# One-head attention of layer 1: batch 0 started inside the last dense steps of layer 0, batches 1 to 3 prepared between its steps

## The reference, cut to what matters

```python
# layer 0, dense part: 8 experts of hidden size 512, top 2 by router, all computed for all tokens
h = gelu(einsum('td,edh->eth', xf, W1) + b1[:, None, :], approximate=False)
expert_out = einsum('eth,ehd->etd', h, W2) + b2[:, None, :]
x = x + einsum('etd,te->td', expert_out, weights)
# layer 1, attention with one head of 128
n = _layernorm(x)
Q = n @ W_q + b_q; K = ctx @ W_k + b_k; V = ctx @ W_v + b_v
x = x + softmax(Q @ K.T * 128 ** -0.5) @ V
# layer 1, dense part: 9 experts of hidden size 256, begins with another _layernorm(x)
```

## Time and profile before

| | before |
|---|---|
| median of 3 runs | 1169.02 us |
| the profiled execution: its own time | 1170.76 us |
| the profiled execution: its span | 1169.0 us |
| mean granted clock of TensorE | 0.908 |
| busy share of the span: TensorE, VectorE, ScalarE, GpSimd | 82%, 53%, 48%, 34% |
| from the first product with keys to the first hidden product of L1f | 350.67 to 380.71 us |

### The profile page before, as it was taken

One profiled execution on the slowest core, in us unless ns is written; L12 is line 12 of the kernel. 1 busy time (PEld: TensorE's weight loads), 2 busy tenths in 40 slices (PEclk: granted clock), 3 DMA queues, 4 the chain that ended last, 5 costly groups with the idle time before them and its releaser, 6 DMA issues. The chain is left out here.

```text
span 1169.0 us, 20619 instructions
## 1 busy us (share of the span) xinstructions
PE 960.7 (82%) x7766; PEld 808.3 (69%) x7766; DVE 621.5 (53%) x1703; ACT 556.4 (48%) x1069; POOL 393.3 (34%) x386
## 2 busy tenths in 40 slices
PE   4888899999997999978898874889377876299992
PEld 3666789999976899955665654889245554288882
DVE  7885421111145443377878765345398775444443
ACT  2665444444435434445666550665345543155552
POOL 4443200100013101410101345356465557545552
PEclk9999899999997999998989895899779986599997
DMA  9999900000000000000000001766200001445543
GB/s 349 189 189 188 205 1 1 2 1 1 1 1 1 1 1 1 1 1 1 2 2 2 19 20 50 229 189 206 81 1 2 1 1 41 146 145 168 172 151 108
DMA packets 70577, 83.83 MB, mean 72 GB/s; under 512 B 5297, under 2 KB 57528, under 8 KB 70352
## 3 DMA queue, kind: packets, MB, share of 16 engines
q1 hardware_dynamic: 64336, 71.98, 25.5%
q0 software_dynamic: 4992, 8.45, 2.1%
q10 hardware_dynamic: 1152, 2.10, 0.5%
HBM read 52.15 MB, written 32.18 MB: 72 GB/s over the span
## 5 line engine op out<-in xcount | busy, mean ns | idle before, releaser
L2283 ACT ACTIVATE hT<-PS,par 128x512 f32<-128x512 f32 x200 | 136.7, 688 | 179.2 <-PE PS L2231 177.6
L2323 DVE SCALAR_TENSOR_TENSOR X<-PS,wts,X 128x128 f32<-128x128 f32 x272 | 76.6, 344 | 226.4 <-PE PS L2243 226.3
L1092 ACT ACTIVATE hT<-PS 116x512 f32<-116x512 f32 (+1 forms) x192 | 102.0, 561 | 103.7 <-PE PS L865 102.4
L865 PE MATMUL PS<-par,score 128*116 128x128 f32 x704 | 109.7, 293 | 24.7 <-DVE oc L996 12.9
L2243 PEld LDWEIGHTS PS<-regA,hT 128*128 128x128 f32 x1024 | 119.2, 192 | 2.8
L2243 PE MATMUL PS<-regA,hT 128*128 128x128 f32 x1024 | 119.4, 275 | 0.0
L865 PEld LDWEIGHTS PS<-par,score 128*116 128x116 f32 x704 | 81.0, 143 | 42.2 <-issue 31.7
L1162 POOL TENSOR_TENSOR score<-score,mx 128x1232 f32<-128x1232 f32 x32 | 72.0, 2251 | 91.1 <-DVE mx L976 91.1
L1997 PE MATMUL PS<-q_up,halves 128*112 128x256 f32 (+1 forms) x276 | 85.6, 310 | 8.8 <-DVE hT L2106 8.8
L2229 PE MATMUL PS<-x_up,w_halves 128*128 128x512 f32 x200 | 86.4, 432 | 0.0
L1069 ACT ACTIVATE score<-score 128x1232 f32<-128x1232 f32 x64 | 78.3, 1223 | 11.8 <-POOL score L1162 9.5
(11 more groups left out here) (313 smaller groups left out, 2021.3 us busy)
## 6 DMA issues: line engine op xcount, KB each, us to landing
regA<-L3f_w SPq DMA_DIRECT2D x23, 704.0 KB, 4.1
regB<-L2f_w SPq DMA_DIRECT2D x23, 578.0 KB, 4.1
L2f_sorted_x<-empty_row SPq DMA_DIRECT2D x8, 1161.0 KB, 20.0
L3f_sorted_x<-empty_row SPq DMA_DIRECT2D x8, 1161.0 KB, 19.5
regA<-L0f_w SPq DMA_DIRECT2D x4, 768.0 KB, 16.9
regA<-L2f_sorted_x SPq DMA_DIRECT2D x23, 129.0 KB, 3.7
regB<-L3f_sorted_x SPq DMA_DIRECT2D x23, 129.0 KB, 4.0
par<-params SPq DMA_DIRECT2D x1, 2450.0 KB, 13.9
```

What stands on the lines that cost most here:

```text
L865: last = nc.tensor.transpose(PS[0:BW, bank_of(("exps", 3 * u + i)), (j % 4) * P:(j % 4) * P + P], exps_of(u)[:, first:first + BW], ident)
L1092: nc.scalar.activation(hT[0:BW, u % 2, i, 0:width], PS[0:BW, bank, 0:width], ACT.Copy).then_inc(pT_ready.sem, 1)
L2283: nc.scalar.activation(hT[:, n % 2, k, :], PS[:, i % 4, :], c["act"], bias=pc(f"{tag}_b1")[:, col:col + 1]).then_inc(h_ready.sem, 1)
```

## The change

Batch 0 is turned ahead of `output(30)` and projected after it. Batch 1 is turned and projected behind the first product with keys, batch 2 in two parts inside the step of batch 0, batch 3 in the step of batch 1. The wait for all four projections is gone, and the projections get four banks (2, 3, 6, 7) instead of two in turn. Of the norm, VectorE still applies groups 0 and 1, now ahead of the statistics in `vector_staggered`; groups 2 and 3 are applied on GpSimd, each behind its reciprocal root. `projections_vector` is no longer called for layer 1. On ScalarE the copies and the projections' evictions of groups 2 and 3 move in between the steps of the attention. Layers 2 and 3 keep their order.

```diff
             def vector_staggered(v, st, g):
                 statistics, apply = vector_functions(v, st)
+                if on_pool and 0 < g < 3:
+                    apply(g - 1)
                 if g < NG:
                     statistics(g)
-                if g:
+                if g and not on_pool:
                     apply(g - 1)
             def pool(p, st):
                 for g in range(taken if before == "attention" else 0, NG):
                     pool_group(p, g)
+                    if on_pool and g >= 2:
+                        p.wait_ge(rstd_ready.sem, rstd_ready.at(g + 1))
+                        for t in range(TG * g, TG * g + TG):
+                            nc.gpsimd.tensor_scalar(xn[:, t, :], X[:, t, :], mv[:, t, 0:1], rstd[:, 0, t:t + 1],
+                                                    ALU.subtract, ALU.mult).then_inc(xn_late.sem, 1)
             def transpose_group(pe, g, at=None):
-                pe.wait_ge(xn_ready.sem, xn_ready.at(TG * (g + 1)))
+                if on_pool and g >= 2:
+                    pe.wait_ge(xn_late.sem, xn_late.at(TG * (g - 1)))
+                else:
+                    pe.wait_ge(xn_ready.sem, xn_ready.at(TG * (g + 1)))
...
             def bank(i):
-                return {"L1x": 2 + i % 2, "L2x": (0 if i < 4 else 4) + i % 2, "L3x": 4 + i % 2}[tag]
+                return {"L1x": (2, 3, 6, 7)[i % 4], "L2x": (0 if i < 4 else 4) + i % 2, "L3x": 4 + i % 2}[tag]
...
-                    elif i >= 2:
+                    elif i >= 2 and tag != "L1x":
                         pe.wait_ge(q_used.sem, q_used.at(i - 1))
...
# single_stage, TensorE
                 scores(0)
+                nm["transpose_group"](pe, 1)
+                pj["tensor_group"](pe, 1)
                 for b in range(B):
+                    if b == 0:
+                        nm["transpose_group"](pe, 2)
                     if b + 1 < B:
                         scores(b + 1)
-                    if b == 0:
-                        pe.wait_ge(q_ready.sem, q_ready.at(B))
                     pe.wait_ge(exp_ready.sem, exp_ready.at(b + 1))
                     for j in range(TG):
                         last = nc.tensor.transpose(PS[0:K, 2 + b % 2, j * P:j * P + P], score[:, b % 2, j, :], ident)
                     last.then_inc(pT_psum.sem, 1)
+                    if b == 0:
+                        pj["tensor_group"](pe, 2)
+                    if b == 1:
+                        nm["transpose_group"](pe, 3)
+                        pj["tensor_group"](pe, 3)
...
# single_stage, ScalarE
                 exps(0)
+                nm["scalar_group"](a, 2)
                 for b in range(B):
                     a.wait_ge(pT_psum.sem, pT_psum.at(b + 1))
                     nc.scalar.activation(hT[0:K, b % 2, 0, :], PS[0:K, 2 + b % 2, :], ACT.Copy).then_inc(pT_ready.sem, 1)
+                    if b == 0:
+                        pj["scalar_group"](a, 2)
+                    if b == 1:
+                        nm["scalar_group"](a, 3)
+                        pj["scalar_group"](a, 3)
...
# ffn_stage, TensorE
                     if n + 1 < steps:
                         hidden(n + 1)
+                    woven = tag == "L0f"
+                    if woven and n == steps - 2:
+                        after_nm["transpose_group"](pe, 0)
                     output(n)
...
-                    if after_nm and n - (steps - NG) >= 2:
+                    if woven and n == steps - 2:
+                        after_nm["project_group"](pe, 0)
+                    if not woven and n - (steps - NG) >= 2:
                         after_nm["transpose_group"](pe, n - (steps - NG) - 2)
-                if after_nm:
+                if not woven:
                     after_nm["tensor_end"](pe)
...
# the list of stages, layer 1
+                        def scalar_head(a, st, nm=nm, pj=pj):
+                            nm["scalar_group"](a, 0)
+                            pj["scalar_group"](a, 0)
+                            nm["scalar_group"](a, 1)
+                            pj["scalar_group"](a, 1)
+
+                        add(dict(scalar=scalar_head, pool=nm["pool"]))
```

More of the change, by code:

```diff
@@ L505, in norm_stage @@
             rstd_ready = sem("rstd", NG)
-            xn_ready = sem("xn", NT)
+            xn_ready = sem("xn", NT - 2 * TG if tag == "L1x" else NT)
             xT_psum = sem("xT_psum", NG)
@@ L513, in norm_stage @@
             shift_ready = sem("minus_mean_by_rstd", NG if on_scalar else 0)
+            on_pool = tag == "L1x"
+            xn_late = sem("xn_late", 2 * TG if on_pool else 0)
             minus_mean, shift = scales[:, 0, :], scales[:, 1, :]
@@ L1191, in attention_stage, with single_stage @@
             return dict(tensor=tensor, vector=vector, scalar=scalar, pool=pool, pool_keys=pool_keys, pool_key_halves=pool_key_halves, pool_spread=pool_spread, x_done=x_done)
-        def single_stage(tag, q_ready, kv, after_nm):
+        def single_stage(tag, q_ready, kv, after_nm, nm, pj):
             scores_ready = sem("scores", B)
@@ L2528, in build @@
                     norm_after_ffn["tensor_end"] = lambda pe, nm=nm, pj=pj: projections_tensor(pe, nm, pj)
-                    add(dict(scalar=lambda a, st, nm=nm, pj=pj: projections_scalar(a, nm, pj),
-                             vector=lambda v, st, nm=nm, pj=pj: projections_vector(v, st, nm, pj), pool=nm["pool"]))
+                    norm_after_ffn["project_group"] = pj["tensor_group"]
+                    if layer == 1:
+                        def scalar_head(a, st, nm=nm, pj=pj):
[4 more added lines that the diff above has]
+                        add(dict(scalar=scalar_head, pool=nm["pool"]))
+                    else:
+                        add(dict(scalar=lambda a, st, nm=nm, pj=pj: projections_scalar(a, nm, pj),
+                                 vector=lambda v, st, nm=nm, pj=pj: projections_vector(v, st, nm, pj), pool=nm["pool"]))
                 if layer >= 2:
@@ L2537, in build @@
                 else:
-                    at = add(single_stage(tag, pj["ready"], kv, next_norm))
+                    at = add(single_stage(tag, pj["ready"], kv, next_norm, nm, pj))
             x_dones.append(at["x_done"])
```

## The result

The changed kernel takes 1162.21 us, the median of seven runs (1159.82 to 1165.25), against 1167.74 for seven runs of the kernel before (1166.87 to 1169.91): a ratio of 0.9946 with an interval of 0.9932 to 0.9960. It is 5.5 us faster. The profiled execution took 1160.29 us, its span is 1158.5.

What follows compares the result with a forecast made beforehand. The prediction saw the chain of norm and projections between dense layer and attention, with no engine full, as what could be saved. Terms +0.9, −5.9, +0.4 and +0.4 made −4.2, from 1169.02 to 1164.8 us; range 1162.4 to 1167.9.

Steps and rivals of the forecast that it cites:

- projection 0 ahead of the last dense addition: Before `output(31)`: projection 0's two matmuls delay the last dense addition by 0.9 us, between 0.4 and 1.0.
- the rest of the way to batch 0: From last dense addition to batch 0's addition to X: the new order saves 5.9 us.
- turning and projection 3 in batch 1: In batch 1's attention step: turning 3 and projection 3 give back 0.4 us of the gain.
- batches 2 and 3, L1f's norm: Behind batch 1: batch steps stay at 4.36 us, and L1f follows in chain from batch 3; no change.
- the clock's return in L1f: At L1f's first hidden products: arriving earlier, TensorE's clock may return late, losing 0 to 2.3 us; 0.4 taken.
- A premise: From attention to L1f: all of L1f follows in chain from batch 3, so time saved there is saved at the end.
- The clock falling for one stretch at the seam: Between dense layer and attention: half clock costs 1.9 us, leaving gain 2.3, 1166.7 us; chance 0.25.
- GpSimd was not late: Rival for GpSimd's groups at the seam: a 1.4 us hold less 0.4 cover, gain 3.2, 1165.8 us; chance 0.06.
- The third rival: Batch 3's transposes and products escape half clock, and 0.4 is not lost later: gain 5.5, 1163.5 us; chance 0.11.
- The fourth rival: Clock falls at the seam until L1f, exposing 8 us of TensorE work: 3.8 slower, 1172.8 us; chance 0.06.

Runs made afterwards that it cites:

- b4: Kernel before with only the four projection banks and the dropped waits, no order changed; ratio 0.9985 to the kernel before.
- a4: Changed kernel with turning 0 and projection 0 issued behind the last dense output; median 1168.41 us, ratio 0.9999 to the kernel before.
- a3: Changed kernel with groups 2 and 3 applied on VectorE, none on GpSimd; median 1167.80 us, ratio 0.9985 to the kernel before.
- b3: Changed kernel with unread spare products on TensorE, seven in L1f's norm and three in the attention; ratio 0.9934 to the kernel before.
- b2: Changed kernel with two extra row sums on VectorE ahead of the additions of batch 3; ratio 0.9935 to the kernel before.
- a2: Changed kernel with the exp table loaded earlier, behind the eviction of projection 0; 1165.27 us, ratio 0.9974 to the kernel before.
- b1: Kernel before, nothing edited, run for a second trace; ratio 1.0003 to the kernel before.
- d1: Changed kernel with ScalarE applying group 3 of L1f's norm ahead of the copies of group 2; median 1177.17 us, ratio 0.9912 to the kernel before.
- c3: Kernel before, nothing edited, run for a third trace; a single execution of 1166.16 us.

## Why the prediction was right or wrong

**The mechanism was right.** The order at the seam is what gained: the projections behind one another were the cost, the waits and banks were not (b4). With the early start undone batch 3 came 2.05 later (a4), with GpSimd's applies undone 3.05 later (a3). The two were undone one at a time, and what they gain may overlap. The weaving of batches 1 to 3 was never undone alone, so its share is not shown.

**The failed step is the sum, with terms mis-sized on one side.** By the distances from step 28:

| term | predicted | measured |
|---|---|---|
| projection 0 ahead of the last dense addition | +0.9 | +0.87 (16.75 to 17.62) |
| the rest of the way to batch 0 | −5.9 | −6.21 (14.43 to 8.22) |
| turning and projection 3 in batch 1 | +0.4 | +0.27 (4.36 to 4.63) |
| batches 2 and 3, L1f's norm | 0 | 0 |
| the clock's return in L1f | +0.4 | +0.12 (130.79 to 130.91) |
| sum | −4.2 | −4.95 |

Each is off by 0.03 to 0.31, and all to the same side. The two largest are the way to batch 0 and the clock's return.

On the way to batch 0 the chain is the one that was foretold, and every leg is a little shorter. Counted from the last dense addition, the eviction of batch 1 ends at 3.79 (foretold 3.9), exp 0 at 5.56 (5.7), the copy of the transposes begins at 6.31 (6.5), and X is reached at 8.22 (8.5).

The term for the clock's return had a wrong price, and this is the step whose reason failed and not only its size. It charged half of the time by which the clock would come back late. The first 6.29 us of L1f, before and changed:

```profile
380.71:387.00 6.29, 5.98 (x26) 4.75 (x27) 5.21 (x17) 4.02 (x6) 2.42 (x3) 0.75 0.01 1
374.86:381.15 6.29, 6.29 (x25) 5.24 (x26) 5.21 (x17) 4.10 (x6) 2.41 (x3) 0.63 0.00 0
```

That is 3.15 and 4.65 us at half clock: the clock did come back 1.5 us later against L1f, for which the prediction's rule charges 0.75, and the layer took only 0.12 longer. In b3 the clock was 1.00 there, TensorE was busy for only 4.54 of the same 6.29 us, and the layer took 130.80. Half clock at the start of L1f cost next to nothing.

A premise was wrong as well and did no harm here: L1f does not follow in chain from batch 3 (b2). Two small slips, 345.75 for 344.6 + 1.07 and 350.7 for 346.35 + 1.17 + 3.34, enter no term of the sum.

**The base was a part of it.** The forecast was worked out from 1169.02, three runs. The seven gave 1167.74, and the 35 of set a spread from 1165.48 to 1172.71. Of the 2.6 us between 1164.8 and 1162.21 the base makes 1.3 and the terms 0.75; the other 0.6 is put down to no stretch. The measured difference, 5.5, would have put the forecast's own base at 1163.5, inside the range. The low end stood 2.4 under the forecast, too near for the scatter of the base and the bias of the terms together.

**What stays open.** 4.95 by one pair of traces is near the measured 5.5, but the old seam alone varies by 1.7 us between executions, so the gain at L1f is 4.6 to 6.3 by the three traces of before, and the later layers add scatter of their own. The ratios of the changed kernel in three sets are 0.9946, 0.9953 and 0.9916; whether the last, on a slower chip, is the same gain was not settled. Nor why a2, a3 and a4 lost more in the medians than at the seam. The spans of the profiled pair differ by 10.5 us, of which 4.95 are the change by the table. Of the other 5.5, 2.4 lie in L2's attention, which differs as much between two executions of an unedited kernel (b1), and 0.8 ahead of step 28; the rest was not traced to anything.

**The rivals.** The clock falling for one stretch at the seam did not happen in the four traces of the changed kernel, at 1.00 from the last dense addition to batch 0. It did in a3, behind an idle 2.33 of TensorE. The Trainium skill (TensorE: Matmul & The Clock Gate, The HAM clock gate) has the slow clock as the default that activity releases. The traces agree: half clock behind the idle 2.33 us of a3, and 0.87 in L1f's norm with the seven spare products of b3 where it was 0.50 without. GpSimd was not late: group 2 was ready 21.1 behind step 28, where 21.5 was foretold; turning 2 waited 0.49 for it, covered by the table load. No hold between GpSimd and VectorE showed either: the small scaling of the last statistics took 0.17 us beside GpSimd's applies. The third rival, a better clock than before, named a gain of 5.5, which is the one measured, and that is chance: its mechanism did not occur. The products with values of batch 3 still took 2.08 at half clock, and the clock came back later against L1f, not sooner. The fourth rival priced an attention at half clock at 8 us of exposed work. The second trace of before shows what it costs in the old order: 0.51 and not 0.79 between batch 0 and batch 3, 0.74 us at batch 3 and 1.24 at L1f. VectorE was busy for 11.26 us in both and covers most of TensorE's work there. The price looks far too high, though no run had the new order at half clock throughout.

## What to carry to other kernels

Measure a local change from a landmark just ahead of it, in several executions: here the seam repeated to 0.01 us in the new order, while the times of the kernel before differed by 7.2 us within one set. A term for the clock needs the engine that carries the stretch first: where ScalarE or VectorE carries most of it, a halved TensorE clock cost little (0.12 us for 1.5 us more of it in L1f, 1.24 for a slow run through three batches), and keeping it up with spare products gained nothing (b3), while a change of the carrying engine's order did (d1). When a chain is shortened, look for what was hidden behind its old length; here it was a table load, worth 0.9 us once it was moved.

## What the runs showed of the hardware that I had not expected

- The same program has different courses in different executions. The kernel before went through its three batches at a mean clock of 0.79, 0.51 and 0.50, and L2's attention took 148.55, 146.29 and 145.78 us with the same instructions.
- A norm of 11.8 us in which TensorE ran at 0.50 throughout, busy for 10.1 of it, was no faster at 0.87 with spare products in it (12.68), and 11.03 at 0.65 without any (c3).
- A dense layer of 130.8 us was as long with 4.65 us of half clock at its start as with 3.15 or none (130.91, 130.79 and 130.80).
- The sets ran on different chips, and the same kernel differs between them: the kernel before has medians of 1169 and 1187 to 1189 us. Of the 13.8 us between the spans of its first two traces 9.0 lie in L2's sparse layer (76.3 and 85.3 us).
